# The first five row tiles of a fused attention and quantized feed-forward kernel in a written-out order

## The chip, the cores and the metric

One Trainium2 chip, one core of it. The metric is the device time of one execution in microseconds. A core has TensorE (PE, matrix products, weight loads shown as PEld), VectorE (DVE), ScalarE (ACT), GpSimd (POOL) and SyncE (SP), which here only issues DMAs. Each engine runs its own list of instructions in order; semaphores join them.

## The reference

```python
x = x + xattn(layernorm(x), ctx_768, Wq, Wk, Wv, Wo, bo)     # x: 8 x 512 x 512, context: 8 x 77 x 384
x = x + ffn(layernorm(x), clip_x, clip_down, w_gate, w_up, w_down)

# xattn: 8 heads of 64; attn = softmax(q k^T / 8); out = attn v; out @ Wo + bo
# ffn:   weights rounded to 8-bit integers per row, activations with one scale over the whole tensor,
#        h = quant(silu(xq Wg^T) * (xq Wu^T)); h Wd^T
```

All inputs and outputs are float32.

## The kernel before

The 4096 rows of x are 32 row tiles of 128; four tiles make one batch of 512 rows. Products in the attention are made from three matmuls of split operands (high and low parts), so each operand is copied to its high half on ScalarE (`split_hi`, line 402) and its low half is a subtraction on VectorE or GpSimd (`split_lo`, line 405).

A setup stage loads the weights and makes the keys. Then come, on line 700 and after, `q_chunk(0, 0..3)`, the queries of batch 0. The program then builds each engine's list by calling small functions; the order of the calls is the order in each engine's queue. The functions that matter:

- `v_rows(r)` (line 384): a value product of 128 context rows on TensorE in one of the two halves of the PSUM tile QO, its high half on ScalarE, its low half on VectorE, and a store on SyncE into the scratch `v_halves`. There are five.
- `load_vb(b)` (line 432): 12 DMA requests on SyncE that read the value blocks of batch b back from `v_halves` into `vbd`.
- `load_xT(b)` (line 243): the transposed input of batch b, 1 MB into the single buffer `xTr`. `q_chunk(b, m)` (line 410) makes a quarter of the queries of batch b from its split halves `xTs`.
- `S(n)` (line 450): scores of tile n, 8 matmuls, into the PSUM tile SP, the same for nearly all tiles; `soft_max`, `soft_sub`, `soft_exp`, `soft_sum`, `soft_rec`, `soft_norm` (lines 474 to 504): the softmax steps, on VectorE, VectorE, ScalarE, VectorE, VectorE, GpSimd. The subtraction reads SP and frees it for S(n + 1).
- `PT(n)` (line 511): five transpositions into PTP; `PT_high`, `PT_low`: their halves on ScalarE and VectorE.
- `PV_rest(b)` and `PV(b, j)` (lines 536, 555): the value product of batch b, in two halves of QO and two of SP, and for each j its halves `os` on ScalarE and VectorE.
- `wo(n)`, `residual(n)` (lines 575, 605): output product in WOP or MI and the sum with x. `first_stats`, `first_aggr`, `first_scale`, `first_bias` (lines 587 to 601): the statistics of x tile n on VectorE, its scale and the sum with bo on GpSimd.
- `w_load(i)`, `w_top`, `w_scale`, `w_inverse`, `w_round`, `w_integer` (lines 663 to 692): one block of 128 feed-forward weight rows is loaded, its largest value taken on VectorE, rounded on ScalarE, made integer on GpSimd and stored. `wraw` has two buffers, so `w_load(i)` waits for `w_integer(i - 2)`. `W_ORDER` (line 655) says which block comes when; four of the 26 are blocks of w_down, 1408 wide instead of 512.

`attend(s)` (line 744) is called for s = 0 to 27 (line 1005) and does, interleaved, the transposition of tile s, the scores and softmax of tile s + 1, the output product of tile s - 5, statistics of tile s + 3 and weight row block s - 1. Its branches for s = 0 to 3 differ in many places from the rest. In attend(4) w_top(3) stands ahead of soft_max(5) on VectorE. After attention comes the feed-forward part, on TensorE from about 345 us on.

Of the kernel before, what the change touches and what calls it, by code (L numbers as in the profile page):

```python
# [62 lines left out]
def block_kernel(nc, x, xT, ctxT, Wq, Wk, Wv, Wo, bo, clip_x, clip_h, w_gate, w_up, w_down, out):  # L63
# [10 lines left out]
    with ctx:  # L74
# [267 lines left out]
        t_kl = {}  # L342
# [41 lines left out]
        def v_rows(r):  # L384
# [4 lines left out]
            last = qo_product(pairs, 512, m, [t_wvl, t_ctxl], lambda bank: [  # L389
                (bank, vst[0:m, r % 2, 0, :], vst[0:m, r % 2, 1, :])], [t_v.get(r - 2)])  # L390
            t_v[r] = dma("sp", vd[r * 128:r * 128 + m], vst[0:m, r % 2], list(last), f"st_v{r % 2}")
# [5 lines left out]
        t_ph = Tokens()  # L397
        t_bn1, t_q, t_oss, t_st2, t_wmx, t_wsc = [Tokens() for _ in range(6)]
# [11 lines left out]
        def q_chunk(b, m):  # L410
            w = slice(m * 128, m * 128 + 128)
            pairs = [(wqs[:, 0, k, w], wqs[:, 1, k, w], xTs[:, 0, k, :], xTs[:, 1, k, :])
                     for k in range(4)]
            if (b, m) == (0, 0):
                at, bank = 0, state["banks"][0]
                state["use"] = 1
                for k in range(4):
                    def fn(e, k=k):
                        e.matmul(bank, pairs[k][0], pairs[k][2], start=(k == 0), stop=False)
                        e.matmul(bank, pairs[k][0], pairs[k][3], start=False, stop=False)  # L420
                        return e.matmul(bank, pairs[k][1], pairs[k][2], start=False, stop=(k == 3))
# [28 lines left out]
        def S(n):  # L450
            b, t = n // 4, n % 4
            w = slice(t * 128, t * 128 + 128)
            if n == 30:
                free = [t_oss[6, 0], t_oss[6, 1]]
            else:
                free = [t_sub[29] if n == 31 else t_sub.get(n - 1)]
            if t == 1 and b > 0:
                free += [t_oss[b - 1, 2], t_oss[b - 1, 3]]

            def fn(e):  # L460
                for j in range(4):
# [4 lines left out]
            t_S[n] = add("pe", fn, [t_q[b], *t_kl, *free], "S_mm")  # L466
# [69 lines left out]
        def PV_rest(b):  # L536

            banks = []
            for j in range(2):
                at = state["use"] % 2  # L540
                state["use"] += 1
                banks.append((at, state["banks"][at], state["free"][at]))
            for k in range(2):
                banks.append((None, SP[:, 512 * k:512 * k + 512], (t_sub[min(4 * b + 4, NT - 1)],)))
            pv_at[b] = banks

            def fn(e):
                for i, (hv, hp) in enumerate(((0, 0), (0, 1), (1, 0))):
                    for j in range(4):
                        q = slice(32 * j, 32 * j + 32)  # L550
                        m = e.matmul(banks[j][1], vbd[q, hv, 4, :], pts[q, hp, 4, :], start=(i == 0), stop=False)
                return m
            add("pe", fn, [t_pl[4 * b + 3], t_vb[b], *(t for bank in banks for t in bank[2])], "qo_mm")

        def PV(b, j):
# [12 lines left out]
            if j < 2:  # L568
                state["free"][at] = (t_oss[b, j],)
# [86 lines left out]
        for at, tile in ((4, 22), (8, 23), (12, 24), (16, 25)):  # L656
            W_ORDER.insert(at, tile)
# [59 lines left out]
        t_pz = add("pool", lambda e: e.memset(PN[:, :, 512:640], 0.0), [t_ctxl, t_wkl], "c_pz")  # L717
        for k in range(4):
            split_hi(1, k)
            split_lo(1, k, ("dve", "pool")[k % 2])  # L720
        v_rows(0)
        S(0)
        soft_max(0)
        soft_sub(0)
        soft_exp(0)
        soft_sum(0)
        soft_rec(0)
        soft_norm(0)
        v_rows(1)
        S(1)  # L730
        soft_max(1)
        soft_sub(1)
        v_rows(2)
        soft_exp(1)
        for n in range(4, XR):
            load_xn(n, [])
        t_sge = add("act", lambda e: e.activation(sge[:, :], clips[:, :], ACT.Exp, scale=-1.0),
                    [t_clip], "sg_e")
        t_sg = add("dve", lambda e: e.tensor_scalar_add(sgp[:, :], sge[:, :], 1.0), [t_sge], "sg_p")
        t_sg = add("dve", lambda e: e.reciprocal(sg[:, :], sgp[:, :]), [t_sg], "sg")  # L740

        DEFER = (1, 2)

        def attend(s):
# [3 lines left out]
                  "pv": t == 0 and b >= 1}  # L748
# [14 lines left out]
            if s < 26 and s != 2:  # L763
# [3 lines left out]
            late_low = s - 1 >= 0 and (s - 1) % 4 in DEFER  # L767
            if t == 0:
# [15 lines left out]
                if 1 <= b:  # L784
# [4 lines left out]
                if s > 0:  # L789
                    S(s + 1)  # L790
                    soft_max(s + 1)
                    soft_sub(s + 1)
                if 1 <= b < NB:
                    load_vb(b)
                PT_high(s)
                if s > 0:
                    soft_exp(s + 1)
# [4 lines left out]
            elif t < 3:  # L802
                if t == 1 and b + 1 < NB and s != 1:
# [13 lines left out]
                if b + 1 < NB:  # L817
                    if t == 2 or s == 1:
                        q_chunk(b + 1, t)
                    if t == 2:  # L820
                        q_chunk(b + 1, 3)
                if s == 2:
                    PT(s)
                    split_hi(2, 0)
                    split_hi(2, 1)
                    PT_high(s)
                    split_hi(2, 2)
                    split_hi(2, 3)
                    first_stats(5)
                    first_aggr(5)  # L830
                    PT_low(s)
                    split_lo(2, 2, "dve")
                    split_lo(2, 3, "dve")
# [4 lines left out]
                if s != 2:  # L838
                    when("x", first_stats, s + 3)
                when("wo", second_stats, s - 5)  # L840
                if t == 2 and 1 <= b and b + 2 < NB:
                    for k in range(4):
                        split_hi(b + 2, k)
                if s != 2:
                    turned()
                if s != 2:
                    when("x", first_aggr, s + 3)
# [3 lines left out]
            else:  # L851
                when("s", S, s + 1)
                when("s", soft_max, s + 1)
                if s > 3:
                    PT_low(s - 1)
                else:
                    v_rows(4)
                    PT(s)
                    PT_high(s)
                when("s", soft_sub, s + 1)  # L860
                if s == 3:
                    PT_low(s)
                when("s", soft_exp, s + 1)
                if s > 3 and b + 2 < NB:
# [7 lines left out]
                if s == 3:  # L872
                    q_chunk(2, 0)
# [3 lines left out]
                if s > 3:  # L877
                    turned()
                when("w", w_inverse, s - 1)
                if s > 3:  # L880
                    PT_low(s)
# [6 lines left out]
            if s == 0:  # L888
                v_rows(3)
            if s == 1:  # L890
                for n in range(3):
                    first_bias(n)
            when("s", soft_norm, s + 1)
            more = t == 2 and b + 2 < NB
            if more:
                for k in range(2 if s == 2 else 3):
# [12 lines left out]
            if t == 3 and 1 <= b and b + 2 < NB:  # L909
                q_chunk(b + 2, 0)  # L910
            if s == 0:
                q_chunk(1, 0)
            if s == 1:
                w_load(2)
# [90 lines left out]
        for s in range(28):  # L1005
            attend(s)
            if s == 1:
                load_vb(0)
            if s == 3:
                t_flat = [t_v[4], t_v[3], t_wol, ("qo_mm", c.count["qo_mm"])]  # L1010
# [424 lines left out]
```

How the kernel before makes its waits and increments, by code:

```python
    def run(self, engine, e):  # L47
        for need, fn, sem, by in self.queue[engine]:
            for s, v in need:
                e.wait_ge(s, v)
            ins = fn(e)
            if sem is not None:
                ins.then_inc(sem, by)
```

## Time and profile before

| | |
|---|---|
| time, median of 3 runs | 546.88 us (546.83 to 549.45) |
| profiled execution, its own time | 546.44 us |
| its span | 544.6 us |
| PE busy | 527.0 us, 97% |
| DVE busy | 475.0 us, 87% |
| ACT busy | 294.0 us, 54% |
| POOL busy | 231.7 us, 43% |

The span is what the trace covers; 1.8 us of the execution's own time lie around it. Shares are means over stages with different limits, so they are read by stage. In the answers of the trace, a line is start, length, engine, source line, operation, written tile <- read tiles, and, in brackets, idle time of the engine before it with what ended it. A length runs to the end of the result, so that the next instruction may start before; the distance of two starts is then what one costs its engine. Lines can be those of a helper (L37 issues a DMA, L223 is the low half of a split, L219 a copy).

### The profile page before, as it was taken

Reading aid. Unit: us, or ns where it says so; the run is one execution under the profiler, and the core shown is the slowest. Engines: PE = TensorE matmul, PEld = TensorE weight load, DVE = VectorE, ACT = ScalarE, POOL = GpSimd, SP = SyncE. Lnnn points to the kernel's source line nnn. Section 1 sums busy time; section 2 is a strip of 40 time slices with the busy share of each in tenths; the row PEclk is TensorE's granted clock in tenths of the full one; section 3 lists DMA queues with packets and bytes.
Section 4 is the critical chain, followed back from the end, with each engine's and each line's share of the span. In section 5 each row is a group of like instructions: output and inputs, shape, how many; then the busy total and the mean of one; then the engine's idle time right before and its main releaser. Section 6 shows DMA issues by size and latency. Waiting matters only on the chain.

```text
span 544.6 us, 8095 instructions
## 1 busy us (share of the span) xinstructions
PE 527.0 (97%) x2733; PEld 356.0 (65%) x2740; DVE 475.0 (87%) x879; ACT 294.0 (54%) x414; POOL 231.7 (43%) x349
## 2 busy tenths in 40 slices
PE   8989889999999999999999899999999999999997
PEld 7868678787888878888788644444444445544444
DVE  4966988999989899898989789999999988899884
ACT  4834545556465654554534656455555533999500
POOL 4386858769596895856553000000000000055442
PEclk9999999999999999999999999999999999999999
DMA  8809375765668465544858954840442110399987
GB/s 310 281 39 300 98 209 172 224 201 179 216 209 270 144 213 180 182 129 163 216 99 293 289 147 212 306 133 11 112 117 45 71 39 7 127 329 231 157 107 128
DMA packets 82943, 93.83 MB, mean 172 GB/s; under 512 B 47085, under 2 KB 50157, under 8 KB 82645
## 3 DMA queue, kind: packets, MB, share of 16 engines
q1 hardware_dynamic: 77877, 84.13, 49.3%
q0 software_dynamic: 4320, 7.87, 9.6%
q10 hardware_dynamic: 704, 1.31, 0.7%
q8 instruction: 22, 0.36, 0.3%
q14 instruction: 20, 0.16, 0.1%
HBM read 47.51 MB, written 37.78 MB: 157 GB/s over the span
## 4 chain that ended last, share of the span: by engine, by line
PE 77%; DVE 12%; DMA 4%; SPq 3%; issue 2%; ACT 1%; POOL 1%; DVEq 0%; POOLq 0%
PE QO L1137 13%; PE SP L1137 13%; PE QO L192 5%; PE QO L194 4%; PE QO L193 4%; PE SP L463 4%; PE PTP L1302 3%; PE QO L1302 3%; PE SP L1302 3%; SPq L37 3%; PE MI L583 2%; PE MI L581 2%; PE MI L582 2%; PE WOP L1302 2%; PE PTP L516 2%
## 5 line engine op out<-in xcount | busy, mean ns | idle before, releaser
L45 POOL DMA_DIRECT2D out<-n2b x30 | 30.3, 1044 | 207.2 <-DVE n2b L1335 207.2
L1144 ACT ACTIVATE sil<-QO,fsc 128x512 f32<-128x512 f32 x87 | 59.8, 687 | 70.7 <-PE QO L1137 69.0
L1137 PE MATMUL QO<-nT,wgu 128*128 128x512 bf16 x340 | 87.3, 379 | 0.6 <-DMA nT<-qb 0.5
L1137 PE MATMUL SP<-nT,wgu 128*128 128x512 bf16 x340 | 87.3, 379 | 0.0
L1148 DVE SCALAR_TENSOR_TENSOR h<-SP,fsc,sil 128x512 f32<-128x512 f32 x87 | 65.1, 748 | 8.9 <-PE SP L1137 7.1
L504 POOL TENSOR_TENSOR PN<-P,rs 128x512 f32<-128x512 f32 x64 | 44.2, 714 | 50.1 <-DVE rs L496 50.1
L1157 DVE TENSOR_REDUCE hmx<-h 128x1 f32<-128x512 f32 x87 | 59.2, 685 | 2.8
L487 ACT ACTIVATE P<-P,r 128x616 f32<-128x616 f32 x32 | 26.0, 811 | 63.6 <-DVE P L483 63.6
L1137 PEld LDWEIGHTS QO<-nT,wgu 128*128 128x128 bf16 x340 | 33.1, 98 | 40.9 <-DMA nT<-qb 1.0
L1137 PEld LDWEIGHTS SP<-nT,wgu 128*128 128x128 bf16 x340 | 33.2, 98 | 40.2 <-DVE h L1148 0.3
L192 PE MATMUL QO<-xTs,wqs 128*128 128x512 f32 x124 | 50.4, 406 | 2.2 <-DVE xTs L223 2.0
L1269 ACT ACTIVATE h<-h,magic,g 128x1536 f32<-128x1536 f32 (+2 forms) x38 | 47.8, 1349 | 3.3 <-DVE g L1073 3.3
L194 PE MATMUL QO<-xTs,wqs 128*128 128x512 f32 x124 | 48.5, 391 | 0.0
L193 PE MATMUL QO<-xTs,wqs 128*128 128x512 f32 x124 | 48.3, 390 | 0.0
L463 PE MATMUL SP<-kst,qs 128*128 128x154 f32 x248 | 38.2, 296 | 3.8 <-DVE os L566 1.8
L602 POOL TENSOR_TENSOR xn<-xn,bob 128x512 f32<-128x512 f32 x32 | 41.3, 1295 | 0.0
L686 ACT ACTIVATE wraw<-wraw,magic,wiv 128x512 f32<-128x512 f32 (+1 forms) x26 | 24.1, 928 | 31.2 <-DVE wiv L679 31.2
L463 PEld LDWEIGHTS SP<-kst,qs 128*128 128x128 f32 x248 | 34.5, 190 | 5.7 <-DVE os L566 2.3
L631 ACT ACTIVATE n<-x,mr,r 128x512 f32<-128x512 f32 x31 | 25.0, 808 | 15.2 <-POOL mr L625 15.2
L1272 DVE TENSOR_SCALAR wgu<-h 128x1536 bf16<-128x1536 f32 (+2 forms) x39 | 29.2, 756 | 1.2 <-ACT h L1269 0.7
L192 PEld LDWEIGHTS QO<-xTs,wqs 128*128 128x128 f32 x124 | 23.3, 188 | 7.7 <-issue 2.2
L493 DVE TENSOR_REDUCE sm<-P 128x8 f32<-128x616 f32 x32 | 25.1, 786 | 2.6 <-ACT P L487 1.6
(224 smaller groups left out, 1202.0 us busy)
## 6 DMA issues: line engine op xcount, KB each, us to landing
xTr<-in_xT SPq DMA_DIRECT2D x8, 1024.0 KB, 7.7
xn<-in_x SPq DMA_DIRECT2D x32, 256.0 KB, 3.7
out<-x SPq DMA_DIRECT2D x32, 256.0 KB, 2.9
n_rows<-n SPq DMA_DIRECT2D x32, 256.0 KB, 2.7
n2b<-n_rows SPq DMA_DIRECT2D x32, 256.0 KB, 3.7
out<-n2b POOLq DMA_DIRECT2D x30, 256.0 KB, 6.6
h_spill<-h SPq DMA_DIRECT2D x2, 2816.0 KB, 9.3
h<-h_spill SPq DMA_DIRECT2D x6, 768.0 KB, 7.1
```

What stands on the lines that cost most here:

```text
L192: e.matmul(ps, lh, rh, start=(i == 0), stop=False)
L193: e.matmul(ps, lh, rl, start=False, stop=False)
L194: m = e.matmul(ps, ll, rh, start=False, stop=(i == n - 1))
L463: m = e.matmul(o, qs[:, b % 2, j, w], kst[:, b, j, :], start=(j % 2 == 0), stop=True, skip_group_check=True)
L504: t_norm[n] = add("pool", lambda e, to=to, rb=rb, l0=l0, l1=l1: e.tensor_tensor(to, u[:, :, l0:l1], rb, ALU.mult), [t_rec[n], t_PT.get(n - ...
L602: t_xb[n] = add("pool", lambda e: e.tensor_tensor(xn[:, n % XR, :], xn[:, n % XR, :], bob[:, :], ALU.add), [t_bn1[n], t_bo], "xb")
L1137: m = e.matmul(ps, wv_[:, k, col:col + 128], nT[:, b % 2, :, k, :], start=(k == 0), stop=(k == 3))
L1144: t_sil[n] = add("act", lambda e: e.activation(sil[:, n % SR, :], gp, ACT.Silu, scale=fsc[:, ic:ic + 1]), [t_g[n], t_fs, t_h.get(n - SR)], ...
L1148: t_h[n] = add("dve", lambda e: e.scalar_tensor_tensor(out=hv, in0=up, scalar=fsc[:, 11 + ic:12 + ic], in1=sil[:, n % SR, :], op0=ALU.mult ...
L1157: t_hm[n] = add("dve", lambda e: e.tensor_reduce(hmx[:, n:n + 1], hv, AX.X, ALU.max, apply_absolute_value=True), [t_h[n]], "hmx")
L1269: a = add("act", lambda e: e.activation(hv, hv, ACT.Identity, bias=magic[:, :], scale=g2[:, 1, 1:2]), [t_g2] + ([t_back[b, p]] if b < 2 el ...
L1302: mm = e.matmul(ps, hq[:, i % 2, k, tt * 128:tt * 128 + 128], wd[:, k, :], start=(k == 0), stop=(k == NI - 1))
```

## The change

The four first row tiles leave `attend`: their steps, with tile 4's scores and softmax, the value product of batch 0, the first q chunk of batch 2 and the weight rows 0 to 2, are written out as one list of calls ahead of the loop, which now runs from s = 4. Every step that was there is still there. What changes places:

- S(0) stands ahead of the first value product; it is issued in two pieces, of which the first needs only q chunk 2 (the same for S(4)).
- `v_rows` is cut into `v_mm` (TensorE) and `v_out` (halves and store), and each goes to its own place.
- The loads of x tiles 4 to 8 and weight rows 0 and 1 are requested ahead of the value stores; `load_vb(0)` and then `load_xT(2)` right behind store 3.
- q_chunk(1, m) stand one by one between the tiles.
- PV_rest(0) stands ahead of S(4), and the value product of batch 0 uses the tiles MI, WOP and both halves of PTP instead of QO and SP. So S(5) no longer waits for `os`, and PT(4) does.
- w_tops(1), w_tops(2), statistics 5 and 6 stand behind the value product.
- The w_down blocks come at places 8, 12, 16 and 20 of `W_ORDER` instead of 4, 8, 12 and 16.

```diff
-            if t == 1 and b > 0:
+            if t == 1 and b > 1:
                 free += [t_oss[b - 1, 2], t_oss[b - 1, 3]]
...
+            if n in (0, 4):
+                add("pe", lambda e: fn(e, 0, 3), [t_qm[b, 2], *t_kl, *free])
+                t_S[n] = add("pe", lambda e: fn(e, 3, 4), [t_q[b]], "S_mm")
+            else:
+                t_S[n] = add("pe", fn, [t_q[b], *t_kl, *free], "S_mm")
...
-            free = t_sub[30] if n == 30 else t_pl[29] if n == 31 else t_pl.get(n - 1)
+            free = t_sub[30] if n == 30 else t_pl[29] if n == 31 else t_oss[0, 1] if n == 4 else t_pl.get(n - 1)
...
-            banks = []
-            for j in range(2):
+            banks = [] if b else [(None, MI[:, :], ()), (None, WOP[:, :], (t_c,)),
+                                  (None, PTP[:, 0:512], ()), (None, PTP[:, 512:1024], ())]
+            for j in range(2 if b else 0):
...
-        for at, tile in ((4, 22), (8, 23), (12, 24), (16, 25)):
+        for at, tile in ((8, 22), (12, 23), (16, 24), (20, 25)):
...
+        for k in range(4):
             split_hi(1, k)
-            split_lo(1, k, ("dve", "pool")[k % 2])
...
+        split_lo(1, 1)
+        split_lo(1, 3)
         for n in range(4, XR):
             load_xn(n, [])
+        w_load(0)
+        w_load(1)
+
+        S(0)
+        v_mm(0)
+        soft(0, "max", "sub", "exp")
         t_sge = add("act", lambda e: e.activation(sge[:, :], clips[:, :], ACT.Exp, scale=-1.0),
                     [t_clip], "sg_e")
+        split_lo(1, 0, "dve")
+        v_out(0)
         t_sg = add("dve", lambda e: e.tensor_scalar_add(sgp[:, :], sge[:, :], 1.0), [t_sge], "sg_p")
         t_sg = add("dve", lambda e: e.reciprocal(sg[:, :], sgp[:, :]), [t_sg], "sg")
+        v_mm(1)
+        S(1)
+        soft(0, "sum", "rec", "norm")
+        soft(1, "max", "sub")
+        v_out(1)
+        v_mm(2)
+        soft(1, "exp")
+        S(2)
+        split_lo(1, 2, "dve")
+        soft(1, "sum", "rec", "norm")
+        first_bias(0)
+        soft(2, "max", "sub")
+        v_out(2)
+        v_mm(3)
+        soft(2, "exp")
+        PT(0)
+        PT_high(0)
+        v_out(3)
+        load_vb(0)
+        t_xT[2] = load_xT(2, t_xTs[1])
+        q_chunk(1, 0)
+        soft(2, "sum", "rec", "norm")
+        first_bias(1)
+        PT_low(0)
+        S(3)
+        row_stats(3)
+        soft(3, "max", "sub")
+        PT(1)
+        PT_high(1)
+        soft(3, "exp")
+        q_chunk(1, 1)
+        PT_low(1)
+        soft(3, "sum", "rec", "norm")
+        first_bias(2)
+        first_bias(3)
+        v_mm(4)
+        v_out(4)
+        t_flat = [t_v[4], t_v[3], t_wol, ("qo_mm", c.count["qo_mm"])]
+        PT(2)
+        PT_high(2)
+        q_chunk(1, 2)
+        PT_low(2)
+        w_tops(0)
+        w_round(0)
+        w_integer(0)
+        w_load(2)
+        PT(3)
+        PT_high(3)
+        q_chunk(1, 3)
+        PT_low(3)
+        row_stats(4)
+        for k in range(4):
+            split_hi(2, k)
+        split_lo(2, 0)
+        split_lo(2, 1)
+        PV_rest(0)
+        S(4)
+        split_lo(2, 2, "dve")
+        soft(4, "max", "sub")
+        split_lo(2, 3, "dve")
+        PV(0, 2)
+        soft(4, "exp")
+        PV(0, 3)
+        soft(4, "sum", "rec", "norm")
+        PV(0, 0)
+        PV(0, 1)
+        w_tops(1)
+        w_round(1)
+        w_integer(1)
+        w_load(3)
+        q_chunk(2, 0)
+        row_stats(5)
+        first_bias(4)
+        w_tops(2)
+        w_round(2)
+        w_integer(2)
+        row_stats(6)
+        first_bias(5)
+        first_bias(6)
...
-        for s in range(28):
+        for s in range(4, 28):
             attend(s)
```

`soft(n, ...)` calls the named softmax steps of tile n; `row_stats(n)` is first_stats, first_aggr and first_scale; `w_tops(i)` is w_top, w_scale and w_inverse. The rest of the diff takes the branches for s under 4 out of `attend`.

## Rows read from the trace of the kernel before

**Rows 1.** The page: granted TensorE clock in 40 slices, tenths of full speed

```profile
PEclk9999999999999999999999999999999999999999
```

**Rows 2.** Waits of TensorE, 25 to 110 us: in total, times, longest

```profile
PE SP L463 <- DVE os L566: 1.8, 1, 1.8
PE SP L463 <- DVE P L483: 1.8, 1, 1.8
PE QO L192 <- DVE xTs L223: 1.1, 1, 1.1
PE QO L551 <- DMA vbd<-v_halves: 1.0, 1, 1.0
```

**Rows 3.** Waits of TensorE, 73.5 to 335 us

```profile
PE QO L192 <- DVE xTs L223: 0.9, 3, 0.3
```

**Rows 4.** Timeline of TensorE: v_rows(0), PV_rest(0), S(6)

```profile
30.34 0.39 PE L192 MATMUL QO<-wvs,cts 128*128 128x512 f32 x1
...
67.18 0.50 PE L551 MATMUL QO<-pts,vbd 32*128 32x512 f32 x2 [0.99 <-DMA vbd<-v_halves]
...
77.37 1.21 PE L463 MATMUL SP<-kst,qs 128*128 128x154 f32 x8
```

**Rows 5.** The chain that ended last, 80 to 83.5 us: start, share of the chain

```profile
81.32 0.55 PE PTP L516 x5
81.87 1.05 PE SP L463 x8
82.92 0.23 PE QO L192
```

**Rows 6.** Timeline of VectorE, 28 to 125 us

```profile
31.70 3.53 DVE L223 TENSOR_TENSOR xTs<-xTr,xTs 128x512 fp32r<-128x512 f32 x2 [3.36 <-ACT xTs L219]
...
66.96 0.63 DVE L670 TENSOR_REDUCE wmx<-wraw 128x1 f32<-128x512 f32 x1
...
67.90 0.68 DVE L588 BATCH_NORM_STATS2 bn<-xn 128x6 f32<-128x512 f32 x1
...
68.70 0.66 DVE L588 BATCH_NORM_STATS2 bn<-xn 128x6 f32<-128x512 f32 x1
...
75.66 0.80 DVE L483 TENSOR_TENSOR P<-SP,mx 128x616 f32<-128x616 f32 x1
...
91.14 0.69 DVE L607 TENSOR_TENSOR x<-MI,xn 128x512 f32<-128x512 f32 x1 [2.31 <-PE MI L583]
...
95.29 0.68 DVE L223 TENSOR_TENSOR xTs<-xTr,xTs 128x512 fp32r<-128x512 f32 x1
```

**Rows 7.** Timeline of ScalarE: four upper halves, one weight rounding

```profile
31.04 2.18 ACT L219 ACTIVATE xTs<-xTr 128x512 fp32r<-128x512 f32 x4
...
70.74 0.82 ACT L686 ACTIVATE wraw<-wraw,magic,wiv 128x512 f32<-128x512 f32 x1 [1.91 <-DVE wiv L679]
```

**Rows 8.** Timeline of GpSimd: low half of Wo, a weight integer, a normalization

```profile
29.46 4.61 POOL L223 TENSOR_TENSOR wos<-wor,wos 128x2048 fp32r<-128x2048 f32 x1
...
68.92 0.62 POOL L692 TENSOR_SCALAR wint<-wraw 128x512 bf16<-128x512 f32 x1 [0.41 <-ACT wraw L686]
...
78.45 1.38 POOL L504 TENSOR_TENSOR PN<-P,rs 128x512 f32<-128x512 f32 x2 [5.84 <-DVE rs L496]
```

**Rows 9.** Timeline of SyncE: third input, value blocks of batch 0, weight row 5

```profile
46.94 0.38 SPq L37 DMA_DIRECT2D xTr<-in_xT  x1
...
56.34 9.49 SPq L37 DMA_DIRECT2D vbd<-v_halves  x12
...
82.03 0.42 SPq L37 DMA_DIRECT2D wraw<-in_ffn_w_gate  x1
```

**Rows 10.** The tile xTr, 15 to 125 us, its four loads

```profile
DMA to landing us min/median/max: 5.5/7.7/8.3
```

**Rows 11.** The chain that ended last, 0 to 120 us: landing of weight row 3

```profile
66.44 3.17 DMA wraw<-in_ffn_w_gate
```

**Rows 12.** DMA issues by line, 15 to 75 us: KB each, median us to landing

```profile
wraw<-in_ffn_w_gate SPq DMA_DIRECT2D x4, 256.0 KB, 4.1
```

More of the change, by code:

```diff
@@ L382, in block_kernel, with v_mm @@
         t_v = Tokens()
-        def v_rows(r):
+        v_at = {}
+        def v_mm(r):
             m = min(128, NB * L - r * 128)
@@ L388, in v_rows, with v_out @@
                      for k in range(3)]
-            last = qo_product(pairs, 512, m, [t_wvl, t_ctxl], lambda bank: [
-                (bank, vst[0:m, r % 2, 0, :], vst[0:m, r % 2, 1, :])], [t_v.get(r - 2)])
-            t_v[r] = dma("sp", vd[r * 128:r * 128 + m], vst[0:m, r % 2], list(last), f"st_v{r % 2}")
+            v_at[r] = qo_bank(pairs, 512, m, [t_wvl, t_ctxl])
+        def v_out(r):
+            m = min(128, NB * L - r * 128)
+            at, bank, t = v_at[r]
+            hi, lo = vst[0:m, r % 2, 0, :], vst[0:m, r % 2, 1, :]
+            th = add("act", lambda e: e.activation(hi, bank, ACT.Copy), [t, t_v.get(r - 2)], "qo_hi")
+            tl = add("dve", lambda e: e.tensor_tensor(lo, bank, hi.bitcast(f32), ALU.subtract),
+                     [th, t_v.get(r - 2)], "qo_lo")
+            state["free"][at] = (tl,)
+            t_v[r] = dma("sp", vd[r * 128:r * 128 + m], vst[0:m, r % 2], [th, tl], f"st_v{r % 2}")
         t_qh, t_S, t_sub, t_PT, t_PV, t_pl, t_Wo = [Tokens() for _ in range(7)]
@@ L542, in PV_rest @@
                 banks.append((at, state["banks"][at], state["free"][at]))
-            for k in range(2):
-                banks.append((None, SP[:, 512 * k:512 * k + 512], (t_sub[min(4 * b + 4, NT - 1)],)))
+            if b:
+                for k in range(2):
+                    banks.append((None, SP[:, 512 * k:512 * k + 512], (t_sub[min(4 * b + 4, NT - 1)],)))
             pv_at[b] = banks
@@ L567, in PV @@
                               [th, *waits], "qo_lo")
-            if j < 2:
+            if at is not None:
                 state["free"][at] = (t_oss[b, j],)
@@ L717, in block_kernel, with soft, row_stats, w_tops @@
         t_pz = add("pool", lambda e: e.memset(PN[:, :, 512:640], 0.0), [t_ctxl, t_wkl], "c_pz")
+        def soft(n, *steps):
+            for step in steps:
+                {"max": soft_max, "sub": soft_sub, "exp": soft_exp, "sum": soft_sum, "rec": soft_rec,
+                 "norm": soft_norm}[step](n)
+        def row_stats(n):
+            first_stats(n)
+            first_aggr(n)
+            first_scale(n)
+        def w_tops(i):
+            w_top(i)
+            w_scale(i)
+            w_inverse(i)
@@ L761, in turned @@
                 PT_high(s)
-            if s < 26 and s != 2:
+            if s < 26:
                 w_load(s)
@@ L802, in attend @@
             elif t < 3:
-                if t == 1 and b + 1 < NB and s != 1:
+                if t == 1 and b + 1 < NB:
                     q_chunk(b + 1, t)
@@ L816, in attend @@
                 when("w", w_inverse, s - 1)
[L817 to L833, printed above, removed]
+                if b + 1 < NB and t == 2:
+                    q_chunk(b + 1, 2)
+                    q_chunk(b + 1, 3)
                 when("w", w_round, s - 1)
@@ L837, in attend @@
                 x_in()
-                if s != 2:
-                    when("x", first_stats, s + 3)
+                when("x", first_stats, s + 3)
                 when("wo", second_stats, s - 5)
-                if t == 2 and 1 <= b and b + 2 < NB:
+                if t == 2 and b + 2 < NB:
                     for k in range(4):
                         split_hi(b + 2, k)
[L844 to L847, printed above, removed]
+                turned()
+                when("x", first_aggr, s + 3)
                 when("wo", second_aggr, s - 5)
@@ L853, in attend @@
                 when("s", soft_max, s + 1)
[L854 to L859, printed above, removed]
+                PT_low(s - 1)
                 when("s", soft_sub, s + 1)
-                if s == 3:
-                    PT_low(s)
                 when("s", soft_exp, s + 1)
-                if s > 3 and b + 2 < NB:
+                if b + 2 < NB:
                     split_lo(b + 2, 3, "dve")
@@ L887, in attend @@
                 when("n2", normed, s - 6)
[L888 to L892, printed above, removed]
             when("s", soft_norm, s + 1)
@@ L895, in attend @@
             if more:
-                for k in range(2 if s == 2 else 3):
+                for k in range(3):
                     split_lo(b + 2, k)
@@ L908, in attend @@
                 when("x", first_bias, s + 3)
-            if t == 3 and 1 <= b and b + 2 < NB:
+            if t == 3 and b + 2 < NB:
                 q_chunk(b + 2, 0)
[L911 to L914, printed above, removed]
         t_nl = {}
```

52 lines of the change are left out of this document (14 added, 38 removed).

## Prediction

> **What bounds the kernel now.** I read the page first. TensorE is busy for 527.0 of 544.6 us, and its granted clock is in the top tenth in every slice [rows 1]. Then I read the waits of TensorE alone, in two stretches. From 25 to 110 us it waits four times for over half a microsecond, 5.7 us together: S(1) for the subtraction of tile 0, q_chunk(2,0) for the split of the third input, PV_rest(0) for the value blocks, S(5) for the two outputs that the value product leaves in the bank SP [rows 2]. From 73.5 to 335 us one more wait is worth naming, 0.9 us in three pieces [rows 3]. So all that this change can win lies between the end of q_chunk(0,3) at 30.34 us and the start of S(6) at 77.37 us [rows 4], and from S(6) on TensorE is the bound: whatever S(6) gains or loses goes into the time one for one.
>
> **How much there is.** The same matrix work stands between these marks before and after. A product matmul starts every 0.23 us, a score group takes 1.05, a transposition group 0.55 [rows 5]. Five value products at 9 x 0.233 = 2.10 make 10.5, six score groups 6.3, five transpositions 2.75, six q chunks at 12 x 0.2275 = 2.73 make 16.4, and the first value product 16 x 0.233 with a slow first one 3.8: 39.7 us. The stretch is 47.03, so 7.3 us are lost (the listed 5.7, short gaps and slow first matmuls behind each gap). That is the most that can be won.
>
> **The change part by part.** I walk the new order through the in-order queues, starting at 30.34. Lengths are those of the rows.
>
> First, S(0) goes ahead of v_mm(0); three of its four matmul pairs need only q chunk 2, and the last waits for the copy of chunk 3, 0.1 us. It ends at 31.5. VectorE has no input split in front of it now: maximum and subtraction at 0.80 each [rows 6] end at 33.3. The wait of S(1) (1.8) goes. Behind the subtraction stands split_lo(1,0). Before, that kind of split began at 31.70, and two of them took 3.53 us although one takes 0.68 elsewhere [rows 6]; GpSimd was in its 4.61 us subtraction until 34.07 [rows 8]. Started at 33.35 I end it at 34.7, 0.6 behind GpSimd's end. The Trainium skill (SBUF — State Buffer, Who interferes with whom) says that a VectorE instruction with two SBUF inputs and a GpSimd instruction that reads SBUF exclude each other, the later one standing until the first is done. By that rule 34.7 is right; by carrying the long duration over with the instruction it would be 36.3.
>
> From there v_out(0) ends at 35.6, and S(1) runs at 35.7. The subtraction of tile 1 ends at 38.6, and split_lo(1,2), which meets the normalization on GpSimd, at 40.1. S(2) and v_mm(3) follow with no gap. q_chunk(1,0) needs the bank of v_mm(2); its lower half leaves VectorE behind sum, maximum and subtraction at 43.3, while TensorE has been ready since 42.55: **lost 0.75**. S(3), PT(1), q_chunk(1,1), v_mm(4), PT(2), q_chunk(1,2), PT(3) and q_chunk(1,3) then run through to 59.1; PT_low(3), which stands behind w_round(0) and PT_high(3) on ScalarE, ends at 58.9, just in time.
>
> Second, SyncE. Loads of xn 4 to 8 and weight rows 0 and 1 move ahead of the value stores, at no cost: nothing is behind them until 35.6, as GpSimd's 34.07, which w_load(0) waits for, is earlier. Store 3 goes out at 45.3, behind it the 12 requests of the value blocks. These take SyncE 9.5 us [rows 9], so they end at 55.4 to 56 and have landed by 57.3, when 59.1 is wanted: the wait for the blocks (1.0) goes, cover 1.8 us. But the third input now stands behind these 12, at 56, where before it was requested at 46.9 [rows 9] and long there. Of the four loads of its kind up to 125 us the quickest landed in 5.5, the median in 7.7 [rows 10]. I take 5.5, since only one small store competes: 61.6.
>
> Third, tile 4. From 59.1 PV_rest(0), S(4) and the four PV run to 63.9 from banks of their own. ScalarE could start split_hi(2,0) at 59.9 but has the input at 61.6; at 0.545 each [rows 7] the third of them is done at 63.3. Then VectorE: split_lo(2,2) to 64.2, maximum, subtraction to 65.8, split_lo(2,3) to 66.4. q_chunk(2,0) waits for that: **lost 2.5**, TensorE 66.5 to 69.2. On VectorE follow two output halves, sum, reciprocal (68.7) and two output halves, to 70.0; the normalization on GpSimd takes 1.38 [rows 8], to 70.1. PT(4) waits for both, the new wait on t_oss[0,1] among them: **lost 0.95**. PT(4), S(5), q_chunk(2,1) run to 74.5. The wait of S(5) on the outputs (1.8) goes, since the bank SP is no longer used.
>
> Fourth, what the moved steps leave behind. Before, weight rows 1 and 2 and the statistics of tiles 5 to 7 were nearly done on VectorE at 69 [rows 6]. Now w_tops(1), statistics 5, w_tops(2), statistics 6 and 7 stand between the last output half and the maximum of tile 5. A weight group takes 0.94, a statistics pair 0.80 [rows 6]: 2 x 0.94 + 2 x 0.80 + 0.60 = 4.1, so 74.0. Then w_top(3), in attend(4), waits for the load of weight row 3. That load waits for w_integer(1): w_tops(1) yields its inverse at 70.9, w_round 0.82 [rows 7], w_integer 0.62 [rows 8], the store ahead on SyncE about 0.4 (a request takes 0.38 [rows 9]), landing 3.17 as before [rows 11]: 76.1. VectorE **stands still for 2.1 us**, and behind it are queued the rest of the weight group (1.0), maximum and subtraction of tile 5 (1.6): 78.8. S(6) waits for that subtraction: **lost 4.3**. Before, it started at 77.37.
>
> Sum: 30.34 + 39.7 + 0.1 + 0.75 + 2.5 + 0.95 + 4.3 = 78.6 by TensorE's side, 78.8 by VectorE's; I take 78.8. So S(6) is **1.4 us later**.
>
> Behind S(6). The value blocks of batch 1 go through SyncE from 77 on, about 10 us, so weight row 5 is requested at 87.5 instead of 82.0 [rows 9] and lands near 91. VectorE wants it at 88.3. Before, it stood still soon behind that step for 2.3 us, until TensorE had done wo(1) [rows 6], and that idle time is the cover; the bound is 0 to 1 us, and I take 0, since the normalization behind it is still 2 us early. The change of W_ORDER moves one 1408-wide weight tile from attend(5) to attend(21), both stretches with no TensorE wait: nothing. Moved biases and scales on GpSimd sit beside waits for normalizations: nothing.
>
> Profiled execution: 546.44 + 1.4 = 547.8. It lies 0.44 under the median of the runs, which becomes 546.88 + 1.4 = **548.3**.
>
> **The rivals.**
> Slower, by the third input: the request behind the 12 takes 7.7 to 8.3 us to land, median and longest of its kind [rows 10]. Everything from split_hi(2,0) on moves by 2.2 to 2.8: 3.6 to 4.2 over before, 550.5 to 551.1. It decides from a landing of 6.8 us. For it: the rows. Against it: at 46.9 five xn loads had gone out just before. Chance 0.20.
> Slower, by VectorE or by the clock: the split started at 33.35 takes what the first of the pair took before, some 2.9 (3.53 less 0.6 for the second), 1.6 more on the whole chain, 549.9; or the weight row wait of 2.1 becomes 3 to 4 with a landing of 4.1 us, the median of its kind [rows 12], 549.2 to 550.2. The longest gap here was 1.8 us and the clock stayed at its upper level of 2.4 GHz [rows 1, 2]; a fall to 1.2 GHz after the 4.3 us wait doubles the work it covers; taken as long as the wait, 4 us more, 552.3. The Trainium skill (TensorE: Matmul & The Clock Gate, Part 1) says that the clock falls when TensorE idles; no row here shows it. Together these have 0.12 beyond 549.6.
> Faster: VectorE is ahead of this walk. The floor is what stands between TensorE and S(6): if the input is in time, the third upper half is done at 61.0, and the same queue gives 76.0, so 545.5, still about no change. Under that one must suppose that the steps overlap more than the lengths show [rows 6]: S(6) at 73.5, 2.5 under the floor, is 543.0. Chance 0.07.
> All seven waits gone, and nothing in their place (the change as it may be meant): S(6) at 30.34 + 39.7 = 70.0, 539.6. It needs w_top(3) not to stand ahead of the maximum of tile 5, which it does. Chance 0.03.
>
> **How the numbers follow.** The forecast case, with its own range of 545.5 to 549.6, has 0.58. The measurement tells about 0.5%, 2.7 us. Faster 0.10, same 0.58, slower 0.32. The range for 8 in 10 runs from 544.6 (under the floor by the doubt in the walk) to 551.6 (above the slow landing).
>
> **What would show it.** S(1) without wait and its subtraction near 38.6; value blocks landed before PV_rest(0), with no wait; the third input requested at 55 to 56, and ScalarE waiting for it; q_chunk(2,0) waiting 2 to 3 us for xTs; VectorE waiting about 2 us for wraw ahead of the maximum of tile 5; S(6) waiting 4 us for the subtraction at P, start near 79. Wrong it is if w_top(3) finds its row there, if the third input lands by 60, or if S(6) starts under 75 or over 82.

## The result, and the profile after

The changed kernel takes 549.89 us (median, 548.45 to 551.1) where the kernel before, in as many runs beside it, takes 546.9 (546.36 to 549.45). The ratio is 1.0041, 95% interval 1.003 to 1.0052: 1.6 to 2.8 us slower by the ratio, 3.0 by the medians. That is inside the range that was given for 8 in 10, but just above the 549.6 at which the forecast case itself ended. The ratio lies under the 0.5% that the measurement was said to tell, its interval reaches just over it. The forecast of 1.4 us more was too small, and it was made of other parts than the time is. The profiled execution of the changed kernel spans 548.2 us, against 544.6.

First the waits of TensorE in the changed kernel, 25 to 110 us (in total, times, longest).

```profile
PE SP L475 <- DVE P L499: 3.7, 1, 3.7
PE QO L192 <- DVE xTs L223: 1.7, 1, 1.7
PE PTP L532 <- POOL PN L520: 0.8, 1, 0.8
PE QO L192 <- DVE vst L398: 0.3, 1, 0.3
```

Of the four waits of [rows 2] three are gone: S(1), the value blocks, and S(5). The fourth, q_chunk(2,0) for the third input's split, grows from 1.1 to 1.7, and new are S(6) for the subtraction of tile 5 (3.7), PT(4) (0.8) and q_chunk(1,0) (0.3): 6.5 us against 5.7.

VectorE of the changed kernel, from its timeline, shows why S(6) waits.

```profile
62.73 0.85 DVE L223 TENSOR_TENSOR xTs<-xTr,xTs 128x512 fp32r<-128x512 f32 x1 [3.19 <-ACT xTs L219]
...
69.19 0.67 DVE L688 TENSOR_REDUCE wmx<-wraw 128x1 f32<-128x512 f32 x1
...
72.73 0.66 DVE L606 BATCH_NORM_STATS2 bn<-xn 128x6 f32<-128x512 f32 x1
75.16 0.69 DVE L688 TENSOR_REDUCE wmx<-wraw 128x1 f32<-128x512 f32 x1 [1.77 <-DMA wraw<-in_ffn_w_gate]
...
76.99 0.80 DVE L499 TENSOR_TENSOR P<-SP,mx 128x616 f32<-128x616 f32 x1
```

It stands still for 3.2 us until ScalarE has made the third upper half of the third input, gets to the left-over weight rows and statistics at 69.19, and then stands still for 1.8 us ahead of weight row 3, with the maximum and the subtraction of tile 5 behind it. TensorE, from its timeline:

```profile
77.84 2.42 PE L475 MATMUL SP<-kst,qs 128*128 128x154 f32 x8 [3.66 <-DVE P L499]
...
83.75 0.40 PE L599 MATMUL WOP<-wos,os 128*128 128x512 f32 x1
```

S(6) starts at 77.84, 0.5 us later than in [rows 4]. But it runs for 2.42 us where it ran for 1.21. The stretches of the same kernel give the reason. Each row has the stretch, its length, the busy times of PE, PEld, DVE, ACT and POOL, then the granted clock, the share of the DMA engines and GB/s.

```profile
72.00:74.00 2.00, 2.00 (x10) 1.49 (x8) 1.36 (x4) 0.82 (x1) 1.87 (x3) 1.00 0.52 114
74.00:76.00 2.00, 0.19 (x1) 0.00 (x0) 0.84 (x3) 0.00 (x0) 1.79 (x4) 1.00 0.42 152
76.00:78.00 2.00, 0.16 (x1) 0.16 (x1) 1.93 (x5) 1.58 (x3) 2.00 (x2) 0.69 0.90 225
78.00:80.00 2.00, 2.00 (x9) 2.00 (x9) 1.52 (x3) 1.11 (x2) 0.98 (x4) 0.50 1.01 383
80.00:82.00 2.00, 2.00 (x7) 1.61 (x6) 1.66 (x3) 0.03 (x1) 1.92 (x4) 0.50 0.91 186
82.00:84.00 2.00, 2.00 (x7) 1.52 (x7) 1.59 (x5) 0.87 (x2) 1.19 (x2) 0.61 0.05 10
84.00:86.00 2.00, 2.00 (x17) 1.86 (x15) 1.35 (x3) 1.43 (x2) 1.88 (x3) 1.00 0.03 7
```

While TensorE stood idle the granted clock fell to 0.50, its lower level of 1.2 GHz, and it came back in 82 to 84 us. In the profiled execution of the kernel before every slice was in the top tenth [rows 1], and its mean granted clock was 1.000. The chain that ended last, for the changed kernel, shows the same as lengths: eight matmuls of wo(0) at 0.43, then 0.23.

```profile
72.20 2.94 DMA wraw<-in_ffn_w_gate
75.14 0.02 issue
75.16 0.69 DVE wmx L688
...
77.84 2.42 PE SP L475 x8
80.27 0.43 PE WOP L599
...
83.92 0.23 PE WOP L599
```

The starts of the score groups in the two timelines of TensorE put a number on each piece:

| start, us | S(1) | S(3) | S(4) | S(5) | S(6) | S(7) | S(9) |
|---|---|---|---|---|---|---|---|
| before | 37.54 | 50.72 | 58.14 | 73.50 | 77.37 | 81.70 | 106.05 |
| after | 35.86 | 46.04 | 60.10 | 70.23 | 77.84 | 85.00 | 109.39 |

At S(5) the changed kernel is 3.3 us ahead, at S(6) 0.5 behind, at S(7) 3.3 behind, and it stays there: from S(9) to the end of the span both take 438.6 to 438.8 us. So the account is: S(6) late by 0.5, and S(6) to S(7) 7.16 us instead of 4.33, 2.8 us of lower clock.

The mean granted clock of every execution is on record, not only of the profiled one. Of the 18 of the changed kernel one had 1.000, and it is the quickest (548.45 us); six had 0.997 (median 549.3), eight 0.993 or 0.994 (549.9), three 0.990 or 0.991 (550.6). The kernel before is not free of it either: of its 71 executions beside the later runs 22 had 0.998 or less, with a median of 548.3 against 546.8 for the other 49. Where in those executions the clock was low only a trace would show.

### The profile page after: what moved, and what is told of

Same layout as the page of the kernel before. It is cut to its first block, busy times and chain, and to the rows that moved or that the text cites. A ratio compares the mean times of both kernels' runs of the same rounds, so it can differ in the third digit from the quotient of the medians.

```text
span 548.2 us, 8100 instructions
## 1 busy us (share of the span) xinstructions
PE 530.1 (97%) x2740; PEld 358.2 (65%) x2740; DVE 472.6 (86%) x879; ACT 294.2 (54%) x414; POOL 230.8 (42%) x349
## 4 chain that ended last, share of the span: by engine, by line
PE 74%; DVE 11%; SPq 6%; DMA 5%; issue 2%; ACT 1%; POOL 0%; ACTq 0%; DVEq 0%; POOLq 0%
PE QO L1200 13%; PE SP L1200 13%; PE QO L192 5%; PE QO L194 4%; PE QO L193 4%; PE SP L475 4%; SPq L37 4%; PE QO L1365 4%; PE PTP L1365 3%; PE SP L1365 3%; DMA v_halves<-vst 2%; SPq L41 2%; PE MI L601 2%; PE MI L599 2%; PE MI L600 2%
## 5 line engine op out<-in xcount | busy, mean ns | idle before, releaser
L475 PE MATMUL SP<-kst,qs 128*128 128x154 f32 x248 | 39.3, 302 | 3.7 <-DVE P L499 3.7
L492 DVE TENSOR_REDUCE mx<-SP 128x8 f32<-128x616 f32 x31 | 24.4, 787 | 4.8 <-PE SP L475 4.6
```

## The experiments

Times are medians; the ratio is that to the kernel before, run beside it. S(n) are starts read from each kernel's timeline of TensorE, as in the table above; they, and what is said of waits and clock, are of one profiled execution each.

| kernel | time | before | ratio, 95% | S(6) | S(7) | S(9) |
|---|---|---|---|---|---|---|
| after | 549.89 | 546.9 | 1.003 to 1.0052 | 77.84 | 85.00 | 109.39 |
| e1_fill | 549.66 | 547.12 | 1.0026 to 1.0058 | 80.20 | 84.54 | 108.92 |
| e2_w3_late | 549.11 | 547.12 | 1.0022 to 1.0046 | 75.03 | 80.81 | 107.87 |
| e3_xT_first | 548.24 | 547.12 | 0.9999 to 1.0025 | 76.72 | 83.51 | 107.90 |
| e4_worder | 547.5 | 547.12 | 0.9994 to 1.0022 | 77.80 | 82.13 | 106.48 |
| e5_fill14 | 548.16 | 546.95 | 0.9997 to 1.0026 | 77.42 | 81.86 | 106.88 |
| e6_early | 547.32 | 546.95 | 0.9987 to 1.0013 | 75.86 | 80.20 | 106.28 |
| e7_spread | 542.19 | 546.95 | 0.9887 to 0.9919 | 73.06 | 77.40 | 101.77 |
| e8_S0_first | 545.33 | 546.95 | 0.9951 to 0.9979 | 76.20 | 80.53 | 104.90 |
| e9b_banks | 550.72 | 547.38 | 1.0062 to 1.0109 | 80.46 | 84.80 | 109.17 |
| e10b_vb_behind | 546.91 | 547.38 | 0.9984 to 1.0002 | 75.76 | 81.52 | 106.93 |

**The clock: filling the wait.** Edit of the changed kernel, in attend:

```diff
                 if t == 1 and b + 1 < NB:
                     q_chunk(b + 1, t)
+                if s == 5:
+                    def fill(e):
+                        for _ in range(28):
+                            m = e.matmul(WOP[:, 0:128], ones[:, :], ones[:, :], start=True, stop=True)
+                        return m
+                    add("pe", fill, [])
                 when("s", S, s + 1)
```

> The changed kernel with 28 small matmuls of constants (into WOP, free at that place) put on TensorE between q_chunk(2,1) and S(6), about 3.1 us of them, inside its wait of 3.66 us. Nothing else is moved and nobody waits for them. Theory: the loss against the kernel before has two terms, S(6) starting 0.5 us late (77.84 against 77.37) and TensorE at its lower clock from 77.84 to 83.7, where S(6) takes 2.42 instead of 1.05 and eight matmuls of wo(0) 0.43 instead of 0.23: 3.0 us. Then the granted clock stays at 1.00 in 70 to 90 us, S(6) still starts near 77.8, and the time is 3.0 us under the changed kernel, within 0.3 of the kernel before plus 0.5: 546.9 to 547.6. Rival (the lower clock comes from the whole stretch with three waits, or the loss is spread behind it): the clock still falls or the time stays above 548.5.

28 of them took 6.2 us, not 3.1, and pushed S(6) itself to 80.20. The granted clock is 1.00 from 70 to 90 us, and S(6) to S(7) took 4.34 us instead of 7.16. So the clock's own price is shown, 2.8 us, but the time says nothing, since S(6) came 2.4 us later. The forecast of the time failed by a length that I had wrongly taken from the transpositions. The next run has `range(14)`.

> The changed kernel with 14 small matmuls between q_chunk(2,1) and S(6) instead of the 28 of the run e1_fill, where 28 took 6.2 us and pushed S(6) itself to 80.20. 14 take 3.1 us and end before the subtraction that S(6) waits for. Theory (S(6) late by 0.5 us, and 2.8 us of lower clock behind it): S(6) at 77.8, S(7) at 82.2 instead of 85.00, S(9) at 106.5 instead of 109.4, time 2.8 us under the changed kernel, 546.8 to 547.6, no different from the kernel before within 0.5 us. Rival (something else behind S(6) takes what the clock gives back, as in e2_w3_late): S(9) at 108 or later, time over 548.5.

From its timeline of TensorE, and one of its stretches:

```profile
73.53 3.29 PE L912 MATMUL WOP<-ones 128*128 128x128 f32 x28
77.42 1.32 PE L475 MATMUL SP<-kst,qs 128*128 128x154 f32 x8 [0.61 <-DVE P L499]
```

```profile
78.00:80.00 2.00, 2.00 (x13) 1.75 (x12) 1.80 (x5) 0.69 (x2) 1.08 (x2) 1.00 1.06 394
```

S(6) at 77.42 and S(7) at 81.86, as forecast, no lower clock there, S(9) 2.5 us sooner than in the changed kernel. The time fell by 1.7 us, to 548.16, where 546.8 to 547.6 was expected: S(9) comes 29.5 us after S(6), not 28.7. The missing 0.8 us is on VectorE. Two lines of its waits at 72 to 112 us, and one of its timeline:

```profile
DVE wmx L688 <- DMA wraw<-in_ffn_w_gate: 3.6, 2, 1.9
DVE bn L606 <- DMA xn<-in_x: 0.6, 1, 0.6
```

```profile
88.58 0.69 DVE L688 TENSOR_REDUCE wmx<-wraw 128x1 f32<-128x512 f32 x1 [1.71 <-DMA wraw<-in_ffn_w_gate]
```

Of the 3.6 us 1.9 are the wait for weight row 3, as in the changed kernel; the other 1.7 are for weight row 5, for which the changed kernel waits 0.2, and S(9) then waits 0.5 us for VectorE. A second weight row is late once TensorE is not. That is the next experiment's subject too.

**Weight row 3 ahead of the maximum of tile 5.** In attend(4) the four steps of weight row 3 go behind the reciprocal of tile 5:

```diff
-                when("w", w_top, s - 1)
+                if s > 4:
+                    when("w", w_top, s - 1)
...
                 when("s", soft_rec, s + 1)
+                if s == 4:
+                    w_tops(3)
+                    w_round(3)
```

> The changed kernel with the steps of weight row 3 (largest value, scale, inverse, rounding) in attend(4) moved behind the softmax steps of tile 5 on VectorE. Theory: maximum and subtraction of tile 5 no longer stand behind the landing of weight row 3, so the subtraction ends near 75.1 and S(6) starts there, 2.7 us sooner; its wait falls from 3.66 to about 1 us, the clock stays up (3.0 more), and the time falls by 5.5 to 6 us, to 543.5 to 544.5. Rival (the third input or the backlog of statistics sets S(6), the weight row is hidden): S(6) starts within 0.5 us of 77.8 and the time stays above 548.

S(6) came at 75.03, as forecast. The time did not follow: S(9) came only 1.5 us sooner, the time 0.8. From the timelines of VectorE and SyncE in this kernel:

```profile
88.99 0.69 DVE L688 TENSOR_REDUCE wmx<-wraw 128x1 f32<-128x512 f32 x1 [3.54 <-DMA wraw<-in_ffn_w_gate]
...
103.34 0.69 DVE L606 BATCH_NORM_STATS2 bn<-xn 128x6 f32<-128x512 f32 x1 [1.90 <-DMA xn<-in_x]
```

```profile
75.93 9.34 SPq L37 DMA_DIRECT2D vbd<-v_halves  x12
85.31 0.51 SPq L37 DMA_DIRECT2D wgu_ints<-wint  x1
85.87 0.42 SPq L37 DMA_DIRECT2D wraw<-in_ffn_w_gate  x1
```

The 12 requests of batch 1 hold SyncE from 75.9 to 85.3, although S(6) came 2.8 us sooner (in the changed kernel from 76.1): they stand behind the request of weight row 4, which waits for w_integer(2). Weight row 5 lands at 89, and VectorE waits for it with the sum of tile 7 behind it. In this execution the clock fell as well, in the wait of q_chunk(2,0) (1.9 us), which put S(5) 0.4 us back. And PT(5) now waits 1.1 us for its normalization. S(6) is no longer what decides; S(9) is.

**The 12 requests behind weight row 5.** The kernel of e2_w3_late, with `load_vb(1)` moved from attend(4) to attend(5), behind `x_in()`.

> The kernel of e2_w3_late (weight row 3 behind the softmax steps of tile 5) with the 12 requests for the value blocks of batch 1 moved on SyncE behind the requests of weight row 5, the first output store and x tile 9, in attend(5). In e2_w3_late S(6) came at 75.0, 2.8 us sooner than in the changed kernel, but S(9) only 1.5 us sooner, with VectorE waiting 3.5 us for weight row 5 and 1.9 us for an x tile. Theory: these two waits come from the 12 requests that stand ahead on SyncE for 9.3 us; then weight row 5 is requested near 80 instead of 85.9, VectorE does not wait for it, and S(9) follows S(6) by 28.7 to 29.5 us as in the kernel before, at 103.7 to 104.6; time 544.5 to 545.6. Rival (VectorE's work itself holds S(9)): S(9) at 107 or later as in e2_w3_late, time over 548.

Weight row 5 was requested at 81.98 and VectorE did not wait for it, and the time fell by 2.2 us against e2_w3_late. But S(9) was at 106.93, not at 104.6 or before, and the time 546.91, not 545.6 or less: the wait for an x tile stayed (1.6 us, now behind the 12 requests), S(6) came 0.7 us later than in e2_w3_late, since q_chunk(2,0) had waited 2.4 us with the clock down behind it, and PT(5) waited 1.1 us. The theory holds for the wait for weight row 5 and fails on the x tile and on S(9), which came 31.2 us after S(6) and not 28.7 to 29.5. The two waits of TensorE that the trace shows there, 1.1 at PT(5) and 0.9 at S(9), are most of that difference.

**The third input ahead of the value blocks.**

```diff
-        load_vb(0)
         t_xT[2] = load_xT(2, t_xTs[1])
+        load_vb(0)
```

> The changed kernel with the third input requested ahead of the 12 requests of the value blocks, not behind them. Theory: the input lands near 51.5, ScalarE starts its upper halves at 59.9 behind the copy of q_chunk(1,3) and not at 61.03, and the whole chain to S(6) moves by 1.1 us; q_chunk(2,0) waits 0.6 instead of 1.7; the value blocks still land before PV_rest(0). S(6) keeps its wait of over 3 us and the clock still falls, so the time is 1.1 us under the changed kernel, 548 to 549. Rival (the input's place behind the value blocks is the main loss): over 2.5 us gained. Rival (the value blocks then come late): PV_rest(0) waits for vbd, time unchanged or longer.

As forecast: the wait of q_chunk(2,0) 0.5 instead of 1.7, no wait for the blocks, S(6) 1.1 sooner with its wait of 3.9 and the clock down, time 548.24. So the place of the third input is worth 1.1 to 1.6 us, not the main part.

**W_ORDER alone**, on the kernel before.

> The kernel before with the new W_ORDER alone (the four wide w_down blocks one place of four later). Theory: both attend(5) and attend(21) hide it, so within 0.3 us of the kernel before. Rival: VectorE, 0.9 us lighter in attend(5), lets S(7) or the residual come sooner, or attend(21) pays: a difference of over 0.5 us either way.

No difference that can be measured (0.9994 to 1.0022). In its profiled execution other waits came out longer (q_chunk(2,0) 2.0 us against 1.1), so S(6) at 77.80 is not a reading of W_ORDER.

**Backlog into the idle time before the third input.** In the changed kernel w_tops(1), w_round(1), w_integer(1), w_load(3), row_stats(5) and row_stats(6) are moved from behind PV(0,1) to ahead of `split_hi(2, k)`.

> The changed kernel with w_tops(1), its rounding and integer, w_load(3) and the statistics of tiles 5 and 6 moved ahead of split_hi(2,*), where VectorE sits idle for 3.2 us until the third input has landed. Theory: nothing but w_tops(2), statistics 7 and w_top(3), landed by then, is left between the last output half and the maximum of tile 5, so S(6) starts at 74.2 to 74.5 with no wait for the subtraction, 3.5 us sooner, and the clock stays up. Behind it SyncE's 12 requests of batch 1 end near 82.6 and weight row 5 lands near 86, 1 to 2 us after VectorE wants it, which costs about 1 us by S(9): S(9) near 104, time 544 to 545.5. Rival (SyncE's 12 requests set S(9) whatever S(6) does, as in e2_w3_late): S(9) at 107 or later, time over 548.

Missed: S(6) at 75.86, S(9) at 106.28, time 547.32, where 74.2 to 74.5, 104 and 544 to 545.5 were expected. The first of its TensorE waits and the timeline of GpSimd:

```profile
PE QO L192 <- POOL xTs L223: 3.1, 1, 3.1
```

```profile
61.23 0.62 POOL L710 TENSOR_SCALAR wint<-wraw 128x512 bf16<-128x512 f32 x1 [0.98 <-ACT wraw L704]
...
63.11 1.00 POOL L616 TENSOR_TENSOR r<-va,mhalf 128x1 f32<-128x1 f32 x1
64.08 2.94 POOL L223 TENSOR_TENSOR xTs<-xTr,xTs 128x512 fp32r<-128x512 f32 x2
```

VectorE had 3.2 us free there, GpSimd 1.3: one weight integer and two scales stood ahead of its two lower halves, which began at 64.08 instead of 61.73. q_chunk(2,0) waited 3.1 us and the clock fell (0.50 in 68 to 70 us). The steps had been counted on one engine of the three that they use. Behind S(6) VectorE waited 3.3 us for weight row 5, as in e2_w3_late.

**Backlog spread.** With what these showed, the changed kernel with w_tops(0) behind v_out(2), w_tops(1) behind the steps of tile 3, w_tops(2) and statistics 4 and 5 behind PT_low(2), statistics 6 behind PT_low(3), and the third input and weight row 2 requested ahead of the value blocks. Parts of the edit:

```diff
         v_out(3)
-        load_vb(0)
         t_xT[2] = load_xT(2, t_xTs[1])
+        w_round(0)
+        w_integer(0)
+        w_load(2)
+        load_vb(0)
...
         PT_high(2)
+        w_round(1)
+        w_integer(1)
+        w_load(3)
         q_chunk(1, 2)
         PT_low(2)
-        w_tops(0)
-        w_round(0)
-        w_integer(0)
-        w_load(2)
+        w_tops(2)
+        w_round(2)
+        w_integer(2)
+        row_stats(4)
+        row_stats(5)
...
```

> The changed kernel with the weight rows and statistics spread over idle time of VectorE: w_tops(0) behind v_out(2), w_tops(1) behind the sum of tile 3, w_tops(2) and statistics 4 and 5 behind PT_low(2), statistics 6 behind PT_low(3); third input and weight row 2 requested ahead of the value blocks of batch 0. Theory: four losses go, the late third input (q_chunk(2,0) waits under 0.7), the backlog and the weight row ahead of the maximum of tile 5 (S(6) at 72.8 to 73.3, no wait), the lower clock, and weight row 5 behind the requests of batch 1 (these can go out from 66 on). S(9) near 101.5 to 102, time 542 to 543, faster than both kernels. Rival (VectorE has too much work up to S(9) for any order): S(9) at 104 or later, time over 544.5.

All as forecast: 542.19 us, ratio 0.9903, S(6) at 73.06, S(9) at 101.77, mean granted clock 1.000 in each of its 6 executions. The waits of TensorE from 28 to 112 us are three; then the request of the value blocks of batch 1 and of weight row 5, on SyncE, 10.6 and 9.2 us sooner than in e2_w3_late.

```profile
PE PTP L532 <- POOL PN L520: 0.8, 1, 0.8
PE QO L192 <- DVE xTs L223: 0.6, 1, 0.6
PE QO L192 <- DVE vst L398: 0.3, 1, 0.3
```

```profile
65.31 10.04 SPq L37 DMA_DIRECT2D vbd<-v_halves  x12
76.25 0.36 SPq L37 DMA_DIRECT2D wgu_ints<-wint  x1
76.65 0.42 SPq L37 DMA_DIRECT2D wraw<-in_ffn_w_gate  x1
```

It is the fastest kernel here, 4.8 us under the kernel before. It takes four losses away together, so it does not show what each was worth.

**Single parts of the change, on the kernel before.** S(0) with its maximum and subtraction ahead of the second input's split and of v_rows(0):

> The kernel before with S(0) and the maximum and subtraction of tile 0 ahead of the second input's split and of the first value product; nothing else of the change. Theory: the wait of S(1) (1.8 us) goes and S(1) starts at 35.7; no other wait takes its place, since TensorE is without a gap up to S(4), so S(6) and S(9) come 1.5 to 1.9 us sooner and the time is 545.0 to 545.6. Rival (the stage is bound further on, by the value blocks behind weight row 0 on SyncE): PV_rest(0) waits the longer, and the time stays within 0.5 us of the kernel before.

545.33 us, ratio 0.9965: this part alone gains 1.6 us (1.1 to 2.7 by the interval). S(9) came 1.15 us sooner, less than the 1.5 that was expected, since S(0), issued in one piece, waited 0.7 us for the copy of q chunk 3. The new banks of the value product, with PT(4) still ahead of S(5) and directly behind the product:

> The kernel before with the value product of batch 0 in MI, WOP and the two halves of PTP alone: S(5) loses its wait for the outputs and PT(4) gets one, as in the change, but PT(4) still stands directly behind the value product and ahead of S(5) on TensorE, with no q chunk between. Theory: the wait only changes its place. PT(4) waits for the last lower half, which ended at 74.5 in the kernel before, and S(5) follows at 75.1 against 73.5; S(6) and S(9) come 1.0 to 1.6 us later, time 548.0 to 548.6. Rival (the banks are the gain of this part whatever the order): S(5) at 72 or sooner, time under 546.

```profile
74.73 1.30 PE L516 MATMUL PTP<-identF,PN 128*128 128x128 f32 x5 [3.42 <-DVE os L568]
```

The wait only changed its place, and it grew: 3.4 us at PT(4), S(5) at 75.82, and the granted clock at 0.53 in 74 to 76 us, which adds 1.3 us by S(6) (PT(4) to S(5) 1.1 instead of 0.55, S(5) to S(6) 4.6 instead of 3.9). 550.72 us, 2.1 over what was expected; the clock, which the expectation left out, is the larger part of that. Its three executions with a mean granted clock of 0.991 to 0.994 took 551.2 to 554.0 us, the three with 0.997 took 549.8 to 550.3. So the new banks do not pay by themselves. In the change, where q_chunk(2,0) stands between the product and PT(4), PT(4) waits 0.8 us, and for the normalization; a kernel that differs in that place alone was not run.

## Why the prediction was right or wrong

**The ceiling: not contradicted. The mark: too early.** The quickest order here gains 4.8 us of the 7.3 that were called the most. But that the time follows S(6) one for one does not hold. In the changed kernel S(6) is 0.5 us late and the time 3.0; in e10b_vb_behind S(6) is 1.6 us sooner than before and the time 0.5 shorter, within the noise; in e2_w3_late S(6) came 2.8 us sooner than in the changed kernel and the time fell by 0.8. The clock and weight row 5 lie between. What the time follows is S(9): from there to the end of the span the twelve profiled executions take 438.3 to 439.3 us.

**The waits that go: right**, all three; so is the reading that S(1) gains (35.86, walk 35.7) and that the value blocks are in time. The waits that come were right in kind, cause and order, and too large: q_chunk(1,0) 0.3 against 0.75, q_chunk(2,0) 1.7 against 2.5, PT(4) 0.8 against 0.95, S(6) 3.7 against 4.3.

**S(6), 78.8 against 77.84: mis-sized by 1.0 us.** ScalarE got the third input at 61.03, not 61.6, and with that the backlog began at 69.2 on VectorE, not at 70.0; weight row 3 landed in 2.94, not 3.17. The walk also adds up wrongly in one place: 70.9 with its four terms 0.82, 0.62, 0.4 and 3.17 is 75.9, not 76.1. The backlog (4.2 us, walked 4.1) and the wait behind it (1.8 against 2.1) were as walked. In the faster rival the third upper half is put at 61.0; from 59.9 at 0.545 each it is 61.5, so that floor is 77.0 and not 76.0. In e3_xT_first, which has the input in time, S(6) started at 76.72.

```profile
61.03 2.20 ACT L219 ACTIVATE xTs<-xTr 128x512 fp32r<-128x512 f32 x4 [1.13 <-DMA xTr<-in_xT]
```

**The clock: the step that failed.** The walk forecast a wait of 4.3 us on TensorE and priced what follows at its usual length; the fall to the lower level stood among the rivals, in a case of 0.12 with two others, at 4 us. It happened in the profiled execution, and cost 2.8 us from S(6) to S(7) (e1_fill and e5_fill14 show 4.3 and 4.4 us there). The profiled executions of e3 and e9b, and those of e2, e6 and e10b behind the wait of q_chunk(2,0), have a fall too. A forecast with a gap of that length should have carried it in its likeliest case. The Trainium skill (TensorE: Matmul & The Clock Gate, Part 1) has the fall at idle. The trace agrees: 0.50 in 78 to 82 us, behind the wait of 3.7. Removing it brought S(9) 2.5 us and the time 1.7 us, since 0.8 us then goes to weight row 5; the last few tenths are within the intervals. That the forecast still came within 1.6 us of the time is in part luck: S(6) was walked 1.0 us too late, and the clock term of 2.8 us was left out, two errors of opposite sign.

**Behind S(6): the cover.** That weight row 5 would cost nothing was right for the changed kernel. But the walk did not have what made it so: the lower clock had slowed TensorE, so that VectorE waited 0.2 us for the row and then 3.6 us for TensorE, as its timeline shows.

```profile
89.07 0.69 DVE L688 TENSOR_REDUCE wmx<-wraw 128x1 f32<-128x512 f32 x1 [0.19 <-DMA wraw<-in_ffn_w_gate]
...
94.45 0.69 DVE L625 TENSOR_TENSOR x<-MI,xn 128x512 f32<-128x512 f32 x1 [3.63 <-PE MI L601]
```

In e5_fill14, at full clock, it cost 0.8 us, inside the bounds of 0 to 1 that were given.

**The rule on two SBUF inputs: right.** split_lo(1,0) started while GpSimd was in the subtraction that ends at 34.18, and ended 0.55 us behind that end; it did not take the 2.9 us along.

```profile
33.42 1.31 DVE L223 TENSOR_TENSOR xTs<-xTr,xTs 128x512 fp32r<-128x512 f32 x1
```

```profile
29.57 4.61 POOL L223 TENSOR_TENSOR wos<-wor,wos 128x2048 fp32r<-128x2048 f32 x1
```

**W_ORDER: right**, nothing measurable. **The slow third input (rival): no**, it was in use 5.7 us after its request at 55.31.

What stays open: the spread of the changed kernel (548.45 to 551.1) goes with the mean granted clock, as the numbers behind the first table show, but no run shows why the fall is longer in one execution than in another. A low clock also need not cost time: in e5_fill14 five executions at 0.996 or 0.997 have a median of 547.9 and seven at 1.000 one of 548.5, in e2_w3_late five and seven have 549.05 and 549.16. And what held S(9) in e10b_vb_behind was not tried one by one.

## What to carry to other kernels

Work that fits nowhere else is not free behind a product: here 4.2 us of it, ahead of the step that frees the next bank, and 1.8 us for a load that it had made late, became a wait of 3.7 us on TensorE. Before a step is moved, count it on each engine that it uses and ask what its DMA stands behind: VectorE's idle 3.2 us were of no use in e6_early because GpSimd had only 1.3, and 12 small requests took SyncE 9.3 us and held one weight row back by 3.9 (85.87 against 81.98). And a gap of 2.4 us or more on TensorE had the lower clock behind it in every trace here: it should be priced with that, 1.3 us in e9b_banks and 2.8 in the changed kernel, or be filled. Last, a wait that is taken away shows what stood behind it, so read on to the point from which the kernels run alike.

## What the runs showed of the hardware

The granted clock fell behind gaps of 1.9 (e2), 2.4, 3.1, 3.4, 3.7 and 3.9 us; it did not fall behind gaps of 1.7 (changed kernel), 1.8 (before) and 2.0 (e4_worder). So near 2 us the length of one gap alone did not decide. At the lower level S(6) took 2.42 us instead of 1.21, and a 128x512 matmul 0.43 instead of 0.23 from start to start.

14 matmuls of 128 columns (float32) took 3.29 us, 0.23 each, where five transpositions of the same width take 0.55, 0.11 each: the one is no measure of the other. The trace shows two records for each of the 14 (x28) and one for each transposition (x5).

The 12 requests for the value blocks took SyncE about 0.78 us each (9.3 us in e2_w3_late), that of a weight row 0.42.
